# A recurrent scan on TensorE: the last 64 state channels packed, and the group norm moved to GpSimd

## The chip, the core and the metric

The kernel runs on one core of a Trainium2 chip. The metric is the time of one execution on the device in microseconds (us), as the median of several runs; lower is better.

## What is computed

The input `x` has 16 images of 56 x 56 pixels with 192 channels. Two blocks follow each other, each added to its input: a window block with a recurrence and a small two-layer network, and then a shifted-window attention block. The change touches only the first, which is, cut down:

```
g   = group_norm(x)                      # 32 groups of 6 channels
w   = layer_norm(windows of 7 x 7 of g) * ln1_w + ln1_b
h_t = w_t @ Bm + h_{t-1} @ A             # over the 49 tokens of a window
r   = h @ Cm
y   = layer_norm(r) * ln2_w + ln2_b
x1  = x + r + gelu(y @ W1 + b1) @ W2 + b2
```

There are 16 x 64 = 1024 windows. Each of the 49 tokens needs the state of the token before it.

## The kernel before

Stage 1 goes through the recurrence in slots. A slot works on one token of half of the windows: four tiles of 128 windows, 512 columns (`NTOK`), with 192 channels split into a part of 128 and a part of 64 (`CB`). With two halves and 49 tokens there are 98 tokens-by-half to do, and they are staggered: slot n computes the state of n+1, the network of n, and the normalised input of n+2. The instructions of each engine stand in the order in which the function `slot` of that engine writes them; engines meet only through semaphores (`wait_ge`, `then_inc`).

Matmuls want more exactness than one pass of the `float32r` format gives, so each operand is split into an upper part (the value as rounded to `float32r`, written by ScalarE) and a lower part (what is left, written mostly by VectorE). A product needs upper by upper, upper by lower and lower by upper. The class `Split` keeps four weight arrays, `a_hi, a_lo` for channels 0 to 127 and `b_hi, b_lo` for the last 64. For the last 64 channels of the data the upper part lies on partitions 0 to 63 and the lower on 64 to 127 of one tile (`hi[:, 1, :]`), and the weights stand there twice, so that one matmul does both. A product by a 192-row weight is thus five matmuls (`terms`), for each block of output columns.

On TensorE a slot is, in order: the scan (L623, 20 matmuls of 512 columns, 10 for the first 128 state channels and 10 for the last 64, into `ps_h`), the transposes of `yb` (L594, L596), the second half of the second layer of n-1 (L608), the first layer (L639, 30 matmuls), the mix `h @ Cm` (L650), the transposes of `xn`, and the first half of the second layer (L608). VectorE makes the lower parts `h_lo`, `y_lo`, `xn_lo` and four of six `g_lo`, the group norm (L505, L507), both layer norms' statistics and the residual sums; GpSimd makes two `g_lo`, the powers `rsa` and `rsb`, the sum `res` and the accumulators `acc_x`, `acc_x2`. SyncE's queue carries, per slot, one load `xt` (L374) and 14 stores of `x1`.

Names of the prediction: `y_lo` and `y_hi` must be complete before the first layer starts (`s_yl`), `xn_lo` and `xn_hi` before the scan (`s_xl`), and `g_lo` before the first half of the second layer (`s_gld`, `s_glp`).

Of the kernel before, what the change touches and what calls it, by code (L numbers as in the profile page):

```python
# [7 lines left out]
fp32 = mybir.dt.float32  # L8
# [15 lines left out]
P = 128  # L24
CB = C - P
# [31 lines left out]
def build(nc, x, A, Bm, Cm, ln1, ln2, W1, b1, W2, b2,  # L57
# [6 lines left out]
    with top:  # L64
# [31 lines left out]
        with ExitStack() as ctx:  # L96
# [8 lines left out]
            W_B, W_A, W_C = (Split(ctx, name, C) for name in ("wB", "wA", "wC"))  # L105
            W_1 = Split(ctx, "w1", HID)
# [8 lines left out]
            with ExitStack() as pre:  # L115
# [34 lines left out]
                def _(act):  # L150
# [9 lines left out]
                    for full, parts in ((fold_B, W_B), (raw_A, W_A), (raw_C, W_C), (fold_1, W_1)):  # L160
                        for t in range(2):
                            act.activation(parts.parts[2 * t][:, :], full[:, t, :], ACT.Copy)
                    act.activation(w2[:, :, 0, :], raw_2[:, :, :], ACT.Copy).then_inc(s_wh, 1)

                @block.gpsimd
                def _(pool):
# [17 lines left out]
                def _(dve):  # L184
# [30 lines left out]

                    dve.wait_ge(s_sum, 1)
# [64 lines left out]
            yb = sb("yb", [P, TPC, C])  # L281
            y_hi, y_lo = sb("y_hi", [P, 2, NTOK], f32r), sb("y_lo", [P, NTOK], f32r)
# [31 lines left out]
            s_t1, s_xh, s_xl = sem("xn_transposed"), sem("xn_hi_ready"), sem("xn_lo_ready")  # L314
            s_scan, s_hh, s_hl = sem("scan_summed"), sem("h_hi_ready"), sem("h_lo_ready")
# [73 lines left out]
            def _(act):  # L389
                act.wait_ge(s_init, 1)  # L390

                def upper_parts(hi, full):
                    act.activation(hi[:, 0, :], full[:, 0, :], ACT.Copy)
                    return act.activation(hi[0:CB, 1, :], full[0:CB, 1, :], ACT.Copy)

                def slot(t, c):
                    n = CHUNKS * t + c
                    if there(n + 1):

                        d = 1 - c  # L400
                        act.wait_ge(s_scan, n + 2)
                        upto(act, s_cm, n)
                        for k, rows in enumerate((P, CB)):
                            last = act.activation(h_hi[d][0:rows, k, :], ps_h[0:rows, k, :], ACT.Identity,  # L404
                                                  bias=hbias[0:rows, k:k + 1])
                        last.then_inc(s_hh, 1)
                    if there(n):
                        act.wait_ge(s_t2, n + 1)
                        upper_parts(y_hi, ps_g).then_inc(s_yh, 1)
# [14 lines left out]
                    if there(n + 2):  # L424
                        act.wait_ge(s_t1, n + 3)
                        upto(act, s_scan, n + 1)
                        upper_parts(xn_hi[c], ps_h).then_inc(s_xh, 1)
# [50 lines left out]
            def _(dve):  # L478
                def lower_parts(hi, lo, full, bias=None):

                    for k, rows, dst in ((0, P, lo[:, :]), (1, CB, hi[CB:P, 1, :])):
                        src, up = full[0:rows, k, :], hi[0:rows, k, :]
                        if bias is None:
                            last = dve.tensor_tensor(dst, src, up, ALU.subtract)
                        else:
                            last = dve.scalar_tensor_tensor(out=dst, in0=src, scalar=bias[0:rows, k:k + 1], in1=up,
                                                            op0=ALU.add, op1=ALU.subtract)
                    return last
# [911 lines left out]
```

## Time and profile before

| | us |
|---|---|
| median of 3 runs (4489.57 to 4497.21) | 4492.04 |
| the profiled execution | 4493.39 |
| its span | 4491.6 |
| TensorE busy, share of the span | 4286.1, 95% |
| VectorE busy | 3938.4, 88% |
| GpSimd busy | 2584.4, 58% |
| ScalarE busy | 2479.7, 55% |

### The profile page before, as it was taken

What the parts mean: (1) busy time and instruction counts of PE and PEld (TensorE: products, weight loads), DVE (VectorE), ACT (ScalarE), POOL (GpSimd) and SP (SyncE); (2) the same over time, 40 slices, a digit from 0 to 9 for tenths busy, and PEclk for the clock granted to TensorE, in tenths of its full rate; (3) what the DMA queues carried; (4) which work ended last, traced back from release to release, by engine and by line L of the source; (5) the groups of instructions that cost most, each with busy time, mean ns of one, the idle gap of its engine ahead of it and who ended that gap; (6) DMA issues with size and microseconds to landing.
All of it is one profiled execution on the core that took longest, in us unless ns stands there. A gap on an engine that the chain in (4) does not pass through costs nothing. (4 is left out here: it accounts for less than half of the span.)

```text
span 4491.6 us, 141866 instructions
## 1 busy us (share of the span) xinstructions
PE 4286.1 (95%) x52040; PEld 3664.5 (82%) x52040; DVE 3938.4 (88%) x8102; ACT 2479.7 (55%) x4852; POOL 2584.4 (58%) x2092
## 2 busy tenths in 40 slices
PE   0699999999999999999996999999999999999999
PEld 0588888888888888888885888888888888888887
DVE  8688888888888888888884999999899899999998
ACT  0244444444444444444442777777777777777776
POOL 0255554445545545555444777777767767777766
PEclk9999999999999999999997999999999999999999
DMA  8011111111111111111111222222222222222222
GB/s 362 23 40 40 40 40 37 38 39 39 39 39 39 39 40 40 40 40 40 37 39 41 78 77 76 76 78 76 77 75 75 76 77 75 77 76 76 79 76 64
DMA packets 390776, 284.66 MB, mean 63 GB/s; under 512 B 148159, under 2 KB 389188, under 8 KB 389700
## 3 DMA queue, kind: packets, MB, share of 16 engines
q1 hardware_dynamic: 387612, 281.57, 21.6%
q10 hardware_dynamic: 3112, 2.39, 0.2%
q8 instruction: 34, 0.56, 0.1%
q14 instruction: 18, 0.15, 0.0%
HBM read 119.00 MB, written 87.31 MB: 46 GB/s over the span
## 5 line engine op out<-in xcount | busy, mean ns | idle before, releaser
L904 POOL TENSOR_TENSOR L<-L,mx 128x588 f32<-128x588 f32 x512 | 600.2, 1172 | 596.1 <-DVE mx L1127 596.1
L608 PE MATMUL ps_o<-w,g_hi 128*128 128x384 f32 x2352 | 710.9, 365 | 5.9 <-DVE g_lo L548 4.1
L418 ACT ACTIVATE gF<-ps_g,b1f 128x512 f32<-128x512 f32 x588 | 406.2, 691 | 393.8 <-PE ps_g L639 391.3
L898 POOL TENSOR_TENSOR E<-E,ri 128x588 f32<-128x588 f32 x512 | 600.2, 1172 | 0.8 <-DVE ri L1133 0.8
L608 PE MATMUL ps_o<-w,g_lo 128*128 128x192 f32 x2352 | 534.3, 254 | 0.0
L447 POOL TENSOR_TENSOR res<-xt,b2b 128x768 f32<-128x768 f32 x98 | 181.0, 1847 | 590.9 <-DVE x L496 590.9
L1189 PE MATMUL ps_s<-Kp,Q 32*64 32x98 f32 x12288 | 493.6, 258 | 21.9 <-issue 18.8
L404 ACT ACTIVATE h_hi<-ps_h,hbias 128x512 fp32r<-128x512 f32 x196 | 123.2, 680 | 703.2 <-PE ps_h L623 703.2
L1011 ACT ACTIVATE o_hi<-ps_v,vb 128x98 fp32r<-128x98 f32 (+1 forms) x1024 | 290.2, 335 | 300.6 <-PE ps_v L1302 292.8
L608 PEld LDWEIGHTS ps_o<-w,g_hi 128*128 128x128 f32 x2352 | 429.3, 189 | 27.1 <-issue 25.1
L608 PEld LDWEIGHTS ps_o<-w,g_lo 128*128 128x128 f32 x2352 | 443.7, 191 | 0.0
L1123 DVE SCALAR_TENSOR_TENSOR L<-ps_s,bias 128x588 f32<-128x588 f32 x512 | 394.7, 771 | 55.0 <-PE ps_s L1189 37.6
L1127 DVE TENSOR_REDUCE mx<-L 128x12 f32<-128x588 f32 x512 | 392.2, 766 | 17.5
L986 ACT ACTIVATE PT<-ps_t 98x588 f32<-98x588 f32 x512 | 343.3, 670 | 112.2 <-PE ps_t L1265 109.2
L1302 PEld LDWEIGHTS ps_v<-PT,Vx 98*32 98x32 f32 x12288 | 310.5, 150 | 93.9 <-issue 64.3
L1131 DVE TENSOR_REDUCE sm<-E 128x12 f32<-128x588 f32 x512 | 386.5, 755 | 0.1
L1189 PEld LDWEIGHTS ps_s<-Kp,Q 32*64 32x64 f32 x12288 | 299.0, 130 | 103.3 <-issue 27.6
L1302 PE MATMUL ps_v<-PT,Vx 98*32 98x49 f32 x12288 | 374.6, 235 | 2.6 <-DVE o_hi L1108 1.3
L457 POOL TENSOR_TENSOR g_lo<-gF,g_hi 128x512 fp32r<-128x512 f32 x196 | 251.0, 1301 | 199.7 <-ACT g_hi L423 199.7
L423 ACT ACTIVATE g_hi<-gF 128x512 fp32r<-128x512 f32 x588 | 355.7, 622 | 0.0
L992 ACT ACTIVATE E<-L 128x588 f32<-128x588 f32 x512 | 351.3, 686 | 3.9 <-POOL L L904 0.8
L541 DVE TENSOR_SCALAR xn<-xn,mva,rsa 128x192 f32<-128x192 f32 x392 | 318.4, 875 | 2.3 <-POOL rsa L452 2.3
(220 smaller groups left out, 12446.9 us busy)
## 6 DMA issues: line engine op xcount, KB each, us to landing
xs<-in_x SPq DMA_DIRECT2D x8, 4704.0 KB, 22.7
xt<-in_x SPq DMA_DIRECT2D x98, 384.0 KB, 3.4
xb<-x_cells SPq DMA_DIRECT2D x128, 294.0 KB
Vx<-V SPq DMA_DIRECT2D x512, 73.5 KB
out<-yo SPq DMA_DIRECT2D x128, 294.0 KB
x_cells<-x SPq DMA_DIRECT2D x780, 48.0 KB
Kp<-K SPq DMA_DIRECT2D x256, 98.0 KB, 2.0
Kp<-K SPq DMA_DIRECT2D x256, 49.0 KB, 2.2
```

What stands on the lines that cost most here:

```text
L418: act.activation(gF[f % 4][:, :], ps_g[:, f % 2, :], ACT.Gelu, bias=b1f[:, f:f + 1]).then_inc(s_gelu, 1)
L423: act.activation(g_hi[:, g, :], gF[g % 4][:, :], ACT.Copy).then_inc(s_gh, 1)
L608: last = pe.matmul(dst, g[:, f, P * k:P * (k + 1)], w, start=(f == 0 and i == 0), stop=(f == FT - 1 and i == 1))
L898: pool.tensor_tensor(e, e, ri[p][:, :].unsqueeze(2).to_broadcast([P, HEADS, T]), ALU.mult)\
L904: pool.tensor_tensor(l, l, mx[p][:, :].unsqueeze(2).to_broadcast([P, HEADS, T]), ALU.subtract).then_inc(s_sub, 1)
L986: act.activation(PT[lp % 2][0:T2, :, :].rearrange("p j (w t) -> p w j t", w=2), ps_t[0:T2, :, 0:JP * SLOT].rearrange("p w (j t) -> p w j t ...
L992: act.activation(E[pp][:, :, :], L[pp][:, :, :], ACT.Exp).then_inc(s_ex, 1)
L1123: dve.scalar_tensor_tensor(out=L[p][:, :, :].rearrange("p (a h) m -> p a (h m)", a=2), in0=ps_s[:, :, 0:SB], scalar=HD ** -0.5, in1=tab, o ...
L1127: dve.tensor_reduce(mx[p][:, :], L[p][:, :, :], AX.X, ALU.max).then_inc(s_mx, 1)
L1131: dve.tensor_reduce(sm[pp][:, :], E[pp][:, :, :], AX.X, ALU.add).then_inc(s_sm, 1)
L1189: last = pe.matmul(s_pair(j)[SLOT * w:SLOT * (w + 1)], Q[c][rows, chunk, 2 * p + w, :], Kp[c][rows, chunk, :, 2 * p + w, :], start=True, s ...
L1302: last = pe.matmul(ps_v[row:row + 2 * HD, col:col + T], Vx[lc][0:T2, 2 * lp + w, g:2 * HD * JP:JP], PT[lp % 2][0:T2, j, T * w:T * (w + 1)] ...
```

## The change

Five things change in stage 1. First, the scan for the last 64 channels: the upper and the lower weights of these 64 output columns stand side by side in one stationary operand of 128 columns (`pack_B`, `pack_A`), so that one matmul gives the product by the upper weights on partitions 0 to 63 of `ps_h[:, 1]` and that by the lower weights on 64 to 127. ScalarE copies the upper half of the partitions into `h_b`, and VectorE adds the two halves. Second, for the first 128 state channels, the lower weights of the last 64 input rows of B and of A are joined in one operand (`W_AB_b_lo`), whose data operand `xh_b` is put together by two ScalarE copies. The scan has 15 matmuls in place of 20, with the packed ones first. Third, the two group-norm operations move from the head of VectorE's slot to the head of GpSimd's. Fourth, lower parts are released one by one, so that the first can start while the second upper part is still being made. Fifth, VectorE's order: `xn` (now L562) goes ahead of `g_lo` 0 and 1, and `g_lo` 4 and 5 go behind the second layer norm's statistics; TensorE takes the first half of the second layer in three pieces, each with its own wait.

```diff
                     if there(n + 1):
 
                         d = 1 - c
-                        pe.wait_ge(s_xl, n + 2)
-                        upto(pe, s_hl, n)
-                        for m, rows in enumerate((P, CB)):
-                            cols = slice(P * m, P * m + rows)
-                            terms = (*W_B.terms(xn_hi[d], xn_lo[d], cols), *W_A.terms(h_hi[d], h_lo[d], cols))
-                            for k, (w, v) in enumerate(terms):
-                                last = pe.matmul(ps_h[0:rows, m, :], w, v, start=(k == 0), stop=(k == len(terms) - 1))
+                        pe.wait_ge(s_xl, 2 * n + 4)
+                        pe.wait_ge(s_xs, n + 2)
+                        upto(pe, s_hl, 2 * n)
+                        upto(pe, s_hs, n)
+                        state = ((W_B, pack_B, xn_hi[d], xn_lo[d]), (W_A, pack_A, h_hi[d], h_lo[d]))
+                        for k, (w, pack, hi, lo) in enumerate(state):
+                            pe.matmul(ps_h[:, 1, :], pack[:, 0, :], hi[:, 0, :], start=(k == 0), stop=False)
+                            pe.matmul(ps_h[0:CB, 1, :], w.parts[0][:, P:C], lo[:, :], start=False, stop=False)
+                            last = pe.matmul(ps_h[:, 1, :], pack[:, 1, :], hi[:, 1, :], start=False, stop=(k == 1))
+                        last.then_inc(s_pack, 1)
+                        cols = slice(0, P)
+                        terms = (*W_B.terms(xn_hi[d], xn_lo[d], cols)[0:4], *W_A.terms(h_hi[d], h_lo[d], cols)[0:4],
+                                 (W_AB_b_lo[:, :], xh_b[d][:, :]))
+                        for k, (w, v) in enumerate(terms):
+                            last = pe.matmul(ps_h[:, 0, :], w, v, start=(k == 0), stop=(k == len(terms) - 1))
                         last.then_inc(s_scan, 1)
...
                     if there(n):
                         upto(pe, s_x1, n)
+                        pe.wait_ge(s_gld, len(LO_DVE) * n + 2)
+                        second_layer(0, (0, 1))
+                        pe.wait_ge(s_glp, len(LO_POOL) * (n + 1))
+                        second_layer(0, LO_POOL)
                         pe.wait_ge(s_gld, len(LO_DVE) * (n + 1))
-                        pe.wait_ge(s_glp, len(LO_POOL) * (n + 1))
-                        second_layer(0).then_inc(s_w2a, 1)
+                        second_layer(0, (4, 5)).then_inc(s_w2a, 1)
...
                     if there(n + 1):
 
                         d = 1 - c
+                        act.wait_ge(s_pack, n + 2)
+                        act.activation(h_b[:, :], ps_h[CB:P, 1, :], ACT.Copy).then_inc(s_hu, 1)
                         act.wait_ge(s_scan, n + 2)
                         upto(act, s_cm, n)
-                        for k, rows in enumerate((P, CB)):
-                            last = act.activation(h_hi[d][0:rows, k, :], ps_h[0:rows, k, :], ACT.Identity,
-                                                  bias=hbias[0:rows, k:k + 1])
-                        last.then_inc(s_hh, 1)
+                        act.activation(h_hi[d][:, 0, :], ps_h[:, 0, :], ACT.Identity,
+                                       bias=hbias[:, 0:1]).then_inc(s_hh, 1)
+                        act.wait_ge(s_hb, n + 2)
+                        act.activation(h_hi[d][0:CB, 1, :], h_b[:, :], ACT.Identity,
+                                       bias=hbias[0:CB, 1:2]).then_inc(s_hh, 1)
...
+                        act.wait_ge(s_xh, 2 * n + 6)
+                        act.activation(xh_b[c][0:CB, :], xn_hi[c][0:CB, 1, :], ACT.Copy).then_inc(s_xs, 1)
+                    if there(n + 1):
+                        act.wait_ge(s_hh, 2 * n + 4)
+                        act.activation(xh_b[1 - c][CB:P, :], h_hi[1 - c][0:CB, 1, :], ACT.Copy).then_inc(s_hs, 1)
...
+                    if there(n + 2):
+
+                        pool.wait_ge(s_x[c], 16 * (t + 2))
+                        upto(pool, s_t1, n + 1)
+                        r = slice(TPC * c, TPC * (c + 1))
+                        pool.tensor_tensor(xn[c][:, :, :], xt[c][:, :, :], R1[:, r, :], ALU.mult).then_inc(s_gs, 1)
+                        pool.wait_ge(s_gs, n + 3)
+                        pool.tensor_tensor(xn[c][:, :, :], xn[c][:, :, :], M1[:, r, :],
+                                           ALU.subtract).then_inc(s_gn, 1)
...
+                        dve.wait_ge(s_hu, n + 2)
+                        dve.tensor_tensor(h_b[:, :], ps_h[0:CB, 1, :], h_b[:, :], ALU.add).then_inc(s_hb, 1)
+                        dve.wait_ge(s_hh, 2 * n + 3)
+                        dve.scalar_tensor_tensor(out=h_lo[d][:, :], in0=ps_h[:, 0, :], scalar=hbias[:, 0:1],
+                                                 in1=h_hi[d][:, 0, :], op0=ALU.add, op1=ALU.subtract).then_inc(s_hl, 1)
+                        dve.wait_ge(s_hh, 2 * n + 4)
+                        dve.wait_ge(s_hb, n + 2)
+                        dve.scalar_tensor_tensor(out=h_hi[d][CB:P, 1, :], in0=h_b[:, :], scalar=hbias[0:CB, 1:2],
+                                                 in1=h_hi[d][0:CB, 1, :], op0=ALU.add, op1=ALU.subtract)\
+                            .then_inc(s_hl, 1)
```

On TensorE, the second half of the scan before: the last two matmuls of 128 state channels and the ten of 64 (partitions x columns of the output stand behind the names).

```order
L623 MATMUL ps_h<-h_hi,wA_b_hi 128x512
L623 MATMUL ps_h<-h_hi,wA_b_lo 128x512
L623 MATMUL ps_h<-xn_hi,wB_a_hi 64x512
L623 MATMUL ps_h<-xn_lo,wB_a_hi 64x512
L623 MATMUL ps_h<-xn_hi,wB_a_lo 64x512
L623 MATMUL ps_h<-xn_hi,wB_b_hi 64x512
L623 MATMUL ps_h<-xn_hi,wB_b_lo 64x512
L623 MATMUL ps_h<-h_hi,wA_a_hi 64x512
L623 MATMUL ps_h<-h_lo,wA_a_hi 64x512
L623 MATMUL ps_h<-h_hi,wA_a_lo 64x512
L623 MATMUL ps_h<-h_hi,wA_b_hi 64x512
L623 MATMUL ps_h<-h_hi,wA_b_lo 64x512
```

The scan of the changed kernel from its first matmul; four more of line L657 follow, the last of them on `xh_b` and `wAB_b_lo`.

```order
L649 MATMUL ps_h<-xn_hi,pack_B 128x512 [waits h_lo_ready,h_b_hi_stacked,xn_b_hi_stacked,xn_lo_ready]
L650 MATMUL ps_h<-xn_lo,wB_a_hi 64x512
L651 MATMUL ps_h<-xn_hi,pack_B 128x512
L649 MATMUL ps_h<-h_hi,pack_A 128x512
L650 MATMUL ps_h<-h_lo,wA_a_hi 64x512
L651 MATMUL ps_h<-h_hi,pack_A 128x512
L657 MATMUL ps_h<-xn_hi,wB_a_hi 128x512
L657 MATMUL ps_h<-xn_lo,wB_a_hi 128x512
L657 MATMUL ps_h<-xn_hi,wB_a_lo 128x512
L657 MATMUL ps_h<-xn_hi,wB_b_hi 128x512
L657 MATMUL ps_h<-h_hi,wA_a_hi 128x512
```

The last 64 channels now come first, in six matmuls, and the output's width changes four times within the scan where it changed once.

On VectorE, the stretch from the mix to the next scan, before: the statistics of the second layer norm (`s6b`, `mvb`, `veb`) and the lower parts that the scan waits for.

```order
L548 TENSOR_TENSOR g_lo<-gF,g_hi 128x512 [waits hidden_hi_ready] x2
L554 BN_STATS s6b<-ps_r 128x6 [waits mixed]
L554 BN_STATS s6b<-ps_r 128x6 x3
L559 BN_AGGR mvb<-s6b 128x2 [waits ln2_stats,weights_loaded]
L559 BN_AGGR mvb<-s6b 128x2 x3
L562 TENSOR_SCALAR veb<-mvb 128x4 [waits ln2_aggregated]
L484 TENSOR_TENSOR xn_lo<-ps_h,xn_hi 128x512 [waits xn_hi_ready]
L484 TENSOR_TENSOR xn_hi<-ps_h,xn_hi 64x512
```

The same stretch of the changed kernel.

```order
L575 BN_STATS s6b<-ps_r 128x6 [waits mixed]
L575 BN_STATS s6b<-ps_r 128x6 x3
L580 BN_AGGR mvb<-s6b 128x2 [waits ln2_stats,weights_loaded]
L580 BN_AGGR mvb<-s6b 128x2 x3
L583 TENSOR_SCALAR veb<-mvb 128x4 [waits ln2_aggregated]
L588 TENSOR_TENSOR g_lo<-gF,g_hi 128x512 [waits hidden_hi_ready] x2
L517 TENSOR_TENSOR xn_lo<-ps_h,xn_hi 128x512 [waits xn_hi_ready]
L517 TENSOR_TENSOR xn_hi<-ps_h,xn_hi 64x512 [waits xn_hi_ready]
```

The pair of `g_lo` moved from ahead of the wait for the mix to behind it, between the statistics and `xn_lo`.

On GpSimd, the head of the changed slot; before, `res` stood directly behind the second `acc_x` row.

```order
L504 TENSOR_TENSOR acc_x<-acc_x,x 128x768
L507 TENSOR_TENSOR acc_x<-acc_x,x1sq 128x768 [waits x1_squared]
L472 TENSOR_TENSOR xn<-xt,R 128x768 [waits xn_transposed,x_loaded0]
L474 TENSOR_TENSOR xn<-xn,M 128x768 [waits gn_scaled]
L481 TENSOR_TENSOR res<-xt,b2b 128x768 [waits x1_ready,gn_scaled]
L486 TENSOR_TENSOR rsa<-vea,neg_half 128x4 [waits ln1_var_eps]
```

Two operations on 768 columns stand between the accumulators and `res`, and the first of them waits for the load of `xt`.

## Rows read from the trace of the kernel before

**Rows 1.** Windows by stage: start, us, busy us (x instructions) per engine, clock, DMA.
```profile
170.00:2385.00 2215.00, 2209.65 (x12972) 1903.54 (x12971) 1957.78 (x4152) 1006.94 (x1747) 1108.76 (x771) 1.00 0.14 38
...
2385.00:4491.00 2106.00, 2044.43 (x38946) 1734.98 (x38945) 1853.83 (x3622) 1463.97 (x3089) 1452.90 (x1295) 0.99 0.27 75
```

**Rows 2.** Waits, 300 to 2100 us: us in total, times, longest.
```profile
DVE xn L505 <- DMA xt<-in_x: 64.5, 79, 1.1
...
PEld ps_g L639 <- DVE y_hi L484: 20.5, 79, 0.3
```

**Rows 3.** Timeline of TensorE, one slot: start, us, engine, line, operation.
```profile
1011.81 0.39 PE L623 MATMUL ps_h<-xn_hi,wB_a_hi 128*128 128x512 f32 x1
...
1016.17 0.39 PE L623 MATMUL ps_h<-h_hi,wA_b_lo 128*64 128x512 f32 x1
...
1016.40 0.60 PE L594 MATMUL ps_g<-ident,yb 128*128 128x128 f32 x4
...
1017.19 0.42 PE L608 MATMUL ps_o<-w,g_hi 128*128 128x384 f32 x1
...
1020.87 0.50 PE L639 MATMUL ps_g<-y_hi,w_a_hi 128*128 128x512 f32 x1
...
1027.90 0.25 PE L650 MATMUL ps_r<-wC_a_hi,h_hi 128*128 128x192 f32 x1
...
1030.00 0.27 PE L650 MATMUL ps_r<-wC_b_lo,h_hi 128*128 128x192 f32 x1
...
1030.11 0.60 PE L594 MATMUL ps_h<-ident,xn 128*128 128x128 f32 x4
...
1031.07 0.44 PE L608 MATMUL ps_o<-w,g_hi 128*128 128x384 f32 x1
...
1034.61 0.39 PE L623 MATMUL ps_h<-xn_hi,wB_a_hi 128*128 128x512 f32 x1
```

**Rows 4.** Timeline of VectorE around the same slot.
```profile
1006.88 1.28 DVE L548 TENSOR_TENSOR g_lo<-gF,g_hi 128x512 fp32r<-128x512 f32 x2
...
1008.08 1.15 DVE L554 BATCH_NORM_STATS2 s6b<-ps_r 128x6 f32<-128x192 f32 x4
...
1010.52 0.68 DVE L484 TENSOR_TENSOR xn_hi<-ps_h,xn_hi 64x512 fp32r<-64x512 f32 x1
...
1014.23 0.56 DVE L496 TENSOR_TENSOR x<-ps_o,x 128x384 f32<-128x384 f32 x1
...
1015.50 1.38 DVE L505 TENSOR_TENSOR xn<-xt,R 128x768 f32<-128x768 f32 x1 [0.71 <-DMA xt<-in_x]
...
1020.13 0.68 DVE L484 TENSOR_TENSOR y_hi<-ps_g,y_hi 64x512 fp32r<-64x512 f32 x1
...
1021.50 0.56 DVE L496 TENSOR_TENSOR x<-ps_o,x 128x384 f32<-128x384 f32 x1
```

**Rows 5.** Timeline of GpSimd, same stretch.
```profile
1010.00 1.01 POOL L461 TENSOR_TENSOR rsb<-veb,neg_half 128x4 f32<-128x4 f32 x1 [3.16 <-DVE veb L562]
...
1014.22 1.85 POOL L473 TENSOR_TENSOR acc_x<-acc_x,x1sq 128x768 f32<-128x768 f32 x1
...
1022.13 1.85 POOL L447 TENSOR_TENSOR res<-xt,b2b 128x768 f32<-128x768 f32 x1 [6.07 <-DVE x L496]
```

**Rows 6.** Timeline of SyncE's DMA queue, and the queue's row of the page.
```profile
1023.10 11.20 SPq L363 DMA_DIRECT2D x_cells<-x  x14
...
1035.00 0.44 SPq L374 DMA_DIRECT2D xt<-in_x  x1
...
xt<-in_x SPq DMA_DIRECT2D x98, 384.0 KB, 3.4
```

**Rows 7.** ScalarE's h_hi: its group on the page, mean ns; then its timeline row.
```profile
L404 ACT ACTIVATE h_hi<-ps_h,hbias 128x512 fp32r<-128x512 f32 x196 | 123.2, 680 | 703.2 <-PE ps_h L623 703.2
...
1016.60 1.26 ACT L404 ACTIVATE h_hi<-ps_h,hbias 128x512 fp32r<-128x512 f32 x2 [7.16 <-PE ps_h L623]
```

**Rows 8.** Line L541, 300 to 2100 us: duration ns min/median/max.
```profile
L541 DVE TENSOR_SCALAR xn<-xn,mva,rsa x315: 373/381/1435, 319.2 to 2099.4; 128x192 f32<-128x192 f32 x158
```

More of the change, by code:

```diff
@@ L162, in _ @@
                             act.activation(parts.parts[2 * t][:, :], full[:, t, :], ACT.Copy)
+                    for full, pack in ((fold_B, pack_B), (raw_A, pack_A)):
+                        for t in range(2):
+                            act.activation(pack[:, t, 0:CB], full[:, t, P:C], ACT.Copy)
                     act.activation(w2[:, :, 0, :], raw_2[:, :, :], ACT.Copy).then_inc(s_wh, 1)
@@ L214, in _ @@
                                                   in1=sq[:, 0, :], op0=ALU.mult, op1=ALU.add))
+                    dve.wait_ge(s_wh, 1)
+                    for full, parts, rows in ((fold_B, W_B, slice(0, CB)), (raw_A, W_A, slice(CB, P))):
+                        dve.tensor_tensor(W_AB_b_lo[rows, :], full[rows, 1, 0:P], parts.parts[2][rows, 0:P],
+                                          ALU.subtract)
                     dve.wait_ge(s_sum, 1)
@@ L281, in build @@
             yb = sb("yb", [P, TPC, C])
+            xh_b = [sb(f"xh_b{b}", [P, NTOK], f32r) for b in range(2)]
+            h_b = sb("h_b", [CB, NTOK])
             y_hi, y_lo = sb("y_hi", [P, 2, NTOK], f32r), sb("y_lo", [P, NTOK], f32r)
@@ L478, in _, with lower_parts @@
             def _(dve):
-                def lower_parts(hi, lo, full, bias=None):
+                def lower_parts(hi, lo, full, upper, count, ready):
                     for k, rows, dst in ((0, P, lo[:, :]), (1, CB, hi[CB:P, 1, :])):
[L482 to L488, printed above, removed]
+                        dve.wait_ge(upper, count + k - 1)
+                        dve.tensor_tensor(dst, full[0:rows, k, :], hi[0:rows, k, :], ALU.subtract).then_inc(ready, 1)
                 def x1_half(b, half, partial, count):
@@ L531, in slot @@
                         dve.tensor_scalar(vea[:, :], mva[:, :, 1], LN_EPS, None, ALU.add).then_inc(s_ve1, 1)
-                    if there(n):
-                        for f in LO_DVE[:2]:
-                            dve.wait_ge(s_gh, FT * n + f + 1)
-                            dve.tensor_tensor(g_lo[:, f, :], gF[f % 4][:, :], g_hi[:, f, :], ALU.subtract)\
-                                .then_inc(s_gld, 1)
-                    if there(n + 2):
                         dve.wait_ge(s_rs1, n + 3)
@@ L597, in transposes, with second_layer @@
                     return last
-                def second_layer(half):
+                def second_layer(half, blocks=range(FT)):
                     for k in (2 * half, 2 * half + 1):
-                        for f in range(FT):
+                        for f in blocks:
                             both = (ps_o[:, k % 2, 0:2 * C], g_hi, w2[:, f, :, :].rearrange("p a c -> p (a c)"))
```

50 lines of the change are left out of this document (26 added, 24 removed).

## The prediction

> **What bounds the kernel now.** I read the windows by stage first [rows 1]. Stage 1, which the change touches, fills 170 to 2385 us, and TensorE is busy for 2209.65 us of that 2215. VectorE has 1957.78, GpSimd 1108.76, ScalarE 1006.94. So a gain has to come out of TensorE's slot, and VectorE is near enough (88%) to take it back. The second stage runs the same instructions before and after, and I give it nothing.
>
> Next, one slot on TensorE's timeline [rows 3]. It runs from the first scan matmul at 1011.81 to the next at 1034.61: 22.80 us. There are 98 of them (x98) [rows 6], so 97 intervals. Inside it: scan 4.59 (to 1016.40), transposes 0.79, second half of the second layer 3.68, first layer 7.03, mix 2.21, transposes 0.96, first half of the second layer 3.54. Twenty scan matmuls in 4.59 is 0.2295 each, start to start.
>
> Two of these pieces contain waits. The second layer takes 3.68 in one half and 3.54 in the other, and the first layer takes 7.03 for 30 matmuls that need 30 x 0.23 = 6.90. That is 0.27 together, and the view of waits names it: weight loads of the first layer waited for `y_hi` 79 times, 0.26 us each [rows 2]. The last lower part ended at 1020.81 [rows 4], the first layer began at 1020.87. The other wait is at the transposes of `xn`, 0.96 against 0.79: the second layer needs `g_lo` 5, which ended at 1008.16 in the slot before [rows 4]. So 22.80 is some 22.36 of matmuls and 0.44 of waits.
>
> **The change, part by part.** I count from the first scan matmul, S = 0.
>
> *Scan.* Fifteen matmuls in place of twenty: 15 x 0.2295 = 3.44, so 1.15 less. A packed matmul is 128 wide, and the width does not change the price: twenty of both widths keep one spacing, the step from 64 wide back to 128 wide included (1016.17 to 1016.40, 0.23) [rows 3]. The change has four changes of width in the scan. Bounds: nothing, by that row; at most a full wait for the matmul ahead, 0.39 - 0.23 = 0.16 each. I take nothing. The Trainium skill, TensorEngine Tiling (Array Packing), Key Properties, says that a change of tiling mode drains TensorE, which would speak against this scan. The row between 64 and 128 wide shows no such gap; by the rule the scan would cost the rival's price below.
>
> *TensorE without a wait.* 3.44 + 0.79 = 4.23; second layer 3.54 to 7.77; first layer 6.90 to 14.67; mix 2.21 to 16.88; transposes 0.79 to 17.67; second layer 3.54 to 21.21. That is the floor, 1.59 under 22.80.
>
> *What is late next.* Between the end of the mix and the next scan TensorE has only 0.79 + 3.54 = 4.33 of work, and VectorE's new order puts everything in there. Before, `g_lo` 4 and 5 stood ahead of the wait for the mix (1006.88 to 1008.08) and cost TensorE 0.17. Now the chain is: the mix's last matmul ends 0.16 after its slot time (1030.00 + 0.27 against 1030.11) [rows 3], 0.05 to get across, then statistics to the end of `xn_hi`, 1008.08 to 1011.20 = 3.12 [rows 4], with the pair of `g_lo` inside, another 1.20, and 0.06 to TensorE (as `y_hi` to the first layer). Sum 4.59, so the next scan starts at 16.88 + 4.59 = 21.47. The last third of the second layer waits for `g_lo` 5 on the way, but that lies within the same time. Of the floor's gain 0.26 goes here.
>
> *The way from scan to first layer.* This was tight before and the change alters it most. The last scan matmul starts at 3.21 and ends at 3.60; `h_hi`'s first part goes from 3.64 (the 0.04 of 1016.56 to 1016.60) to 4.32 [rows 7]. VectorE comes from its last sum, which ended 3.59 after `xn_hi` (1011.20 to 1014.79) [rows 4], at 3.53 here; it adds `h_b` to 4.21, and `h_lo` ends at 5.11 (three lower parts take 1017.86 to 1020.13, 0.76 each [rows 4, 7]). ScalarE's `h_b` copy (0.68 at most, by `h_hi`'s mean) fits between the packed part, over at 1.54, and 3.53. Then comes the lower part of the last 64 channels, L539. Both its inputs lie in SBUF, and GpSimd will be in the group norm. When is that? `x1`'s second half ends 1.33 behind the second layer (1022.06 against 1020.73) [rows 3, 4], so at 9.10; the load `xt` is issued 12.94 later (1035.00, behind 14 stores of 11.20) and lands in 3.4 [rows 6]: 25.44, which is 3.8 in the next slot. The accumulators end 6.07 after `rsb` starts (1010.00 to 1016.07) [rows 5]; that is about 3.5. So the first norm operation runs from 3.9 to 5.75 if it takes 1.85, as `acc_x2` does [rows 5]. Bounds: 1.38, VectorE's own time for it, to 2.4 if VectorE holds it up by 0.55.
>
> What happens when they meet is in the rows. L505 read two SBUF tiles and started at 1015.50 under GpSimd's `acc_x2`, which ended at 1016.07; it ended at 1016.88, 0.81 later [rows 4, 5]. Likewise L541 has a median of 381 ns and a maximum of 1435 [rows 8]. So I let L539 wait for the norm's end and then take 512/768 of 0.81: 5.75 + 0.54 = 6.29. `y_lo` and `y_hi` follow to 7.7, against 7.77 when TensorE wants them. The Trainium skill, SBUF — State Buffer, Who interferes with whom, has the same as a rule: a VectorE instruction with two SBUF inputs contends with a GpSimd one that reads SBUF, and the second to issue blocks until the first is done. The trace agrees by that 0.81; a reader who thought of port sharing as a slight slowdown would put L539 at 5.9 and see no danger. The 0.27 wait for `y_hi` is thus just gone, with nothing to spare. I put 0.1 for it and 0.08 for restarts of TensorE after its wait at the scan.
>
> *Hidden.* The norm on GpSimd is up to 3.7 in place of VectorE's 2.4; it sits in GpSimd's idle 6.07 before `res` [rows 5] and ends by 7.6 to 8.2, ahead of the statistics at 9.1. Without that cover `xn` would be late by the excess. `res` then runs 9.17 to 11.02, `rsa` to 12.1, the four `xn` (now with GpSimd idle, 0.38 each at most) to 13.6, `g_lo` 0 and 1 (1.28 for a pair) to 15.0; TensorE needs them at 17.67. The fifth gelu waits for `g_lo` 0 until 14.3 instead of 13.7; its upper part is wanted at about 18.9. The two `xh_b` copies on ScalarE come after `xn_hi` is transposed (18 plus 4 x 0.68 = 20.7), before 21.5. Filling the pipeline costs some longer GpSimd steps and the packing of weights six small operations: 3 us once.
>
> *Sum.* 21.47 + 0.18 = 21.65 a slot, 1.15 less than 22.80. 97 x 1.15 = 112; the profiled execution's 4493.4 - 112 + 3 = 4384. It stood 1.4 above the median of the runs, so 4383 there.
>
> **Rivals.**
> *No wait left (0.10).* The chain behind the mix may be shorter than I add up, since it was taken with gaps of other waits in it. Then the floor holds: 97 x 1.59 = 154, 4493.4 - 154 + 3 - 1.4 = 4341. Against it: statistics, `g_lo` and `xn` lower parts are 4.3 of pure work.
> *The scan drains at changes of width (0.10).* 2 changes more a slot than before (four and none behind it, against one and one) at 0.16 is 0.32 with everything behind it: 97 x 0.32 = 31, so 4414. For it: a packed and a 64-wide matmul in one accumulation do not occur in this trace. Against: the 0.23.
> *The state's lower part misses its gap (0.10).* If the first norm operation ends before L539 is ready at 5.11, the second takes the port for 1.85. With an end at 5.3 and L539 later still (a late `h_hi`): 7.15, L539 to 7.7, `y_hi` to 9.1, first layer at 9.2 instead of 7.77, slot 9.2 + 6.90 + 2.21 + 4.59 + 0.15 = 23.05. That is 0.25 longer than before: 97 x 0.25 = 24, and 4516. It decides at 0.64 us, the distance from 5.11 to 5.75; a load landing that much earlier or a state that much later does it. This is the slower case. Another 0.03 goes to slower by a wait I don't see.
> *The gain is eaten to within 0.2% (0.05):* a mixture of late `y_hi` and late `g_lo`, slot 22.75.
>
> **How the numbers follow.** My forecast, 4365 to 4410, has 0.62. The measurement of this kernel tells about 0.2% (9 us) from no change. Faster: 0.62 + 0.10 + 0.10 = 0.82; same 0.05; slower 0.13. The range 4345 to 4440 takes in the forecast, the drain at twice its price and most of the way to the floor.
>
> **What the profile of after would show.** Scan matmuls 0.23 apart across widths, or gaps of 0.16 there. A slot of 21.65. TensorE idle by 0.2 to 0.4 ahead of the last third of the second layer and of the scan, `xn` lower parts ending just before the scan. L539 at 1.1 to 1.3 us, ending 0.54 after the first norm operation. `xn` (L562) at 0.38 throughout. The first norm operation starting 3.8 after the scan. If L539 ends after the second norm operation and the first layer waits over 1 us for `y_hi`, the slower rival holds; if TensorE has no waits, the floor does.

## The result, and the profile after

The changed kernel takes 4386.88 us (median of 4 runs, 4384.31 to 4396.41) against 4490.81 us in the runs beside it: a ratio of 0.977, with a 95% interval of 0.9751 to 0.9788. The prediction said 4383. The profiled execution took 4384.42 us, where the prediction's sum had 4384. One of the six executions of e8 below, at 13239.63 us, is left out as slow.

The head of its page: the span, then busy us, share and instructions of each engine.

```profile
span 4382.6 us, 142449 instructions
...
PE 4170.2 (95%) x51550; PEld 3612.2 (82%) x51550; DVE 3617.6 (83%) x8006; ACT 2658.1 (61%) x5150; POOL 3076.1 (70%) x2292
```

VectorE fell from 88% to 83%, GpSimd rose from 58% to 70%, TensorE stayed at 95%. The windows by stage, cut where stage 1 ends now, answer to [rows 1].

```profile
175.00:2282.00 2107.00, 2096.51 (x12473) 1853.56 (x12474) 1635.36 (x4057) 1182.77 (x2034) 1588.64 (x961) 1.00 0.15 40
2282.00:4382.00 2100.00, 2040.67 (x38957) 1730.98 (x38956) 1854.50 (x3622) 1461.24 (x3089) 1453.06 (x1295) 0.99 0.27 75
```

The second stage takes what it took. TensorE is still busy in nearly all of stage 1. The slot's length can be read from the starts of one scan matmul; this row is line L649 between 300 and 2100 us (count, duration in ns, first and last start).

```profile
L649 PE MATMUL ps_h<-xn_hi,pack_B x83: 466/473/504, 300.1 to 2082.2; 128*128 128x512 f32 x83
```

82 intervals between 300.1 and 2082.2 us make 21.73 us a slot, where it was 22.81. The two halves of the loop now differ: slots of about 21.6 and 21.86 us take turns. One slot on TensorE's timeline, to lay beside [rows 3]:

```profile
995.58 0.47 PE L649 MATMUL ps_h<-xn_hi,pack_B 128*128 128x512 f32 x1
995.89 0.39 PE L650 MATMUL ps_h<-xn_lo,wB_a_hi 128*64 128x512 f32 x1
996.12 0.39 PE L651 MATMUL ps_h<-xn_hi,pack_B 128*128 128x512 f32 x1
996.35 0.39 PE L649 MATMUL ps_h<-h_hi,pack_A 128*128 128x512 f32 x1
...
999.10 0.60 PE L620 MATMUL ps_g<-ident,yb 128*128 128x128 f32 x4
...
999.89 0.42 PE L634 MATMUL ps_o<-w,g_hi 128*128 128x384 f32 x1
...
1003.40 0.39 PE L673 MATMUL ps_g<-y_hi,w_a_hi 128*128 128x512 f32 x1
...
1012.50 0.60 PE L620 MATMUL ps_h<-ident,xn 128*128 128x128 f32 x4
...
1013.29 0.42 PE L634 MATMUL ps_o<-w,g_hi 128*128 128x384 f32 x1
...
1015.55 0.25 PE L634 MATMUL ps_o<-w,g_lo 128*128 128x192 f32 x1
1015.82 0.44 PE L634 MATMUL ps_o<-w,g_hi 128*128 128x384 f32 x1
...
1017.14 0.50 PE L649 MATMUL ps_h<-xn_hi,pack_B 128*128 128x512 f32 x1
```

The four changes of width in the scan leave no gap: 995.89, 996.12 and 996.35 lie 0.23 apart through 64, 128 and 128 columns. Only the first matmul behind a wait is slow (995.58 to 995.89, 0.31; at 1017.14, in the other half of the loop, 0.34). The scan takes 3.52, transposes 0.79, the second half of the second layer 3.51, first layer and mix 9.10. In the first half of the second layer the third piece starts at 1015.82, 0.27 behind its last neighbour instead of 0.09, and the next scan at 1017.14. The view of waits puts names to the two (us in total, times, longest):

```profile
PEld ps_o L634 <- DVE g_lo L588: 20.7, 82, 0.3
PEld ps_h L649 <- issue: 13.5, 42, 0.4
PEld ps_h L649 <- DVE xn_hi L517: 6.7, 41, 0.2
```

`g_lo` 5 costs the weight loads 0.25 a slot. The scan's weight loads wait 0.16 for `xn_hi` in one half of the loop. In the other they stand idle for 0.32, put down to "issue", which is time for which the profile shows no cause. VectorE over the same slot, answering to [rows 4]:

```profile
1000.02 0.75 DVE L535 SCALAR_TENSOR_TENSOR h_lo<-ps_h,hbias,h_hi 128x512 fp32r<-128x512 f32 x1 [0.48 <-ACT h_hi L421]
1000.80 0.92 DVE L539 SCALAR_TENSOR_TENSOR h_hi<-h_b,hbias,h_hi 64x512 fp32r<-64x512 f32 x1
...
1002.47 0.68 DVE L517 TENSOR_TENSOR y_hi<-ps_g,y_hi 64x512 fp32r<-64x512 f32 x1
1003.60 0.56 DVE L522 TENSOR_TENSOR x<-ps_o,res 128x384 f32<-128x384 f32 x1 [0.45 <-PE ps_o L634]
...
1007.91 1.25 DVE L562 TENSOR_SCALAR xn<-xn,mva,rsa 128x192 f32<-128x192 f32 x4 [1.13 <-POOL rsa L486]
...
1012.70 1.16 DVE L575 BATCH_NORM_STATS2 s6b<-ps_r 128x6 f32<-128x192 f32 x4 [2.33 <-PE ps_r L684]
...
1014.47 1.29 DVE L588 TENSOR_TENSOR g_lo<-gF,g_hi 128x512 fp32r<-128x512 f32 x2
...
1016.40 0.68 DVE L517 TENSOR_TENSOR xn_hi<-ps_h,xn_hi 64x512 fp32r<-64x512 f32 x1
```

And GpSimd, answering to [rows 5]:

```profile
997.51 1.86 POOL L507 TENSOR_TENSOR acc_x<-acc_x,x1sq 128x768 f32<-128x768 f32 x1
999.33 1.83 POOL L472 TENSOR_TENSOR xn<-xt,R 128x768 f32<-128x768 f32 x1
1001.24 2.17 POOL L474 TENSOR_TENSOR xn<-xn,M 128x768 f32<-128x768 f32 x1
...
1009.48 3.29 POOL L491 TENSOR_TENSOR g_lo<-gF,g_hi 128x512 fp32r<-128x512 f32 x2 [1.60 <-ACT g_hi L442]
1014.62 1.41 POOL L495 TENSOR_TENSOR rsb<-veb,neg_half 128x4 f32<-128x4 f32 x1 [1.86 <-DVE veb L583]
```

These rows show the two engines at the port that they share. L539 was ready at 1000.80 while GpSimd's L472 ran to 1001.16; it ended at 1001.72, 0.56 behind it. In turn L474 started under L539 and took 2.17, where it takes 1.83 to 1.86 in e4 and e6, and `rsb`, which began under two `g_lo`, took 1.41 where it took 1.01. `h_lo` (L535), with one input from PSUM, ran wholly under L472 and took 0.75, as it does with GpSimd idle in e6. `xn` runs in 1.25 in place of 3.25; GpSimd is idle then (1007.88 to 1009.48), where it was in `g_lo` before. `y_hi` ended at 1003.15, 0.25 before the first layer at 1003.40: no wait there. L472 followed directly on `acc_x2` (997.51 + 1.86); between 300 and 2100 us it waited for the load of `xt` in two slots, for 0.4 us in all.

### The profile page after: what moved, and what is told of

Its sections match the earlier page's. It is cut to its first block and busy times, and to the rows that moved or that the text cites. A ratio compares the mean times of both kernels' runs of the same rounds, so it can differ in the third digit from the quotient of the medians.

```text
span 4382.6 us, 142449 instructions
## 1 busy us (share of the span) xinstructions
PE 4170.2 (95%) x51550; PEld 3612.2 (82%) x51550; DVE 3617.6 (83%) x8006; ACT 2658.1 (61%) x5150; POOL 3076.1 (70%) x2292
## 5 line engine op out<-in xcount | busy, mean ns | idle before, releaser
L634 PE MATMUL ps_o<-w,g_hi 128*128 128x384 f32 x2352 | 722.9, 367 | 5.3 <-DVE g_lo L588 1.9
L491 POOL TENSOR_TENSOR g_lo<-gF,g_hi 128x512 fp32r<-128x512 f32 x196 | 314.2, 1622 | 172.7 <-ACT g_hi L442 172.7
L575 DVE BATCH_NORM_STATS2 s6b<-ps_r 128x6 f32<-128x192 f32 x392 | 113.5, 352 | 235.8 <-PE ps_r L684 235.8
L1302 PE MATMUL ps_t<-ident,E 64*98 64x64 f32 x6144 | 277.5, 223 | 0.0
```

Source lines behind the costliest of these rows:

```text
L634: last = pe.matmul(dst, g[:, f, P * k:P * (k + 1)], w, start=(f == 0 and i == 0), stop=(f == FT - 1 and i == 1))
L1302: last = pe.transpose(ps_t[0:T2, w, SLOT * j:SLOT * (j + 1)], E[lp][rows, 2 * j:2 * j + 2, :].rearrange("p h m -> p (h m)"), ident[rows, r ...
```

## The experiments

Each slot below is read as for the changed kernel, from the first and last start of a scan matmul between 300 and 2100 us. The runs fall in three groups, each with its own runs of the kernel before: 4490.26 us for e1 to e4, 4493.15 for e5 to e8, 4493.76 for e9 and e10. Every ratio is to the group's own; a difference of 3 us across groups means nothing.

| run | what is different | us | slot, us |
|---|---|---|---|
| before | | 4490 to 4494 | 22.81 |
| changed | | 4386.9 | 21.73 |
| e1 | norm at the head of VectorE's slot | 4528.2 | 23.28 |
| e2 | changed, with the scan of 20 matmuls | 4487.7 | 22.77 |
| e3 | `g_lo` 4 ahead of the mix | 4399.6 | 21.83 |
| e4 | 0.69 us more before L539 | 4590.7 | 23.87 |
| e5 | `g_lo` 5 on GpSimd | 4381.6 | 21.69 |
| e6 | norm waits for L539 | 4388.9 | 21.75 |
| e7 | e5 and e6 together | 4341.2 | 21.24 |
| e8 | no 64-wide matmul in the scan | 4389.8 | 21.75 |
| e9 | e7 with the scan of 20 | 4448.4 | 22.40 |
| e10 | e5, and the norm on VectorE behind `y_hi` | 4426.8 | 22.16 |

### e1: the norm back on VectorE

```diff
 (GpSimd's slot)
-                    if there(n + 2):
-
-                        pool.wait_ge(s_x[c], 16 * (t + 2))
-                        ...
 (head of VectorE's slot)
+                    if there(n + 2):
+
+                        dve.wait_ge(s_x[c], 16 * (t + 2))
+                        upto(dve, s_t1, n + 1)
+                        r = slice(TPC * c, TPC * (c + 1))
+                        dve.tensor_tensor(xn[c][:, :, :], xt[c][:, :, :], R1[:, r, :], ALU.mult).then_inc(s_gs, 1)
+                        dve.wait_ge(s_gs, n + 3)
+                        dve.tensor_tensor(xn[c][:, :, :], xn[c][:, :, :], M1[:, r, :],
+                                          ALU.subtract).then_inc(s_gn, 1)
```

> The changed kernel with the two group-norm operations back at the head of VectorE's slot; all the rest as changed. Theory P (a slot is TensorE's matmuls plus the waits that the chains through ScalarE and VectorE leave): the norm cannot start before xt lands, 3.75 us after the scan begins, and h_b, h_lo, h_hi, y_lo, y_hi stand behind it on VectorE, so y_hi ends at about 9.3 instead of 7.6 and the first layer waits about 1.5. Slot about 23.1 us, time about 4520 us: slower than the kernel before, although its scan has five matmuls fewer. Rival Q (the packed scan is worth its five matmuls wherever the norm stands, since VectorE has over 10% of idle time): slot about 21.7 to 21.9, time 4385 to 4405.

4528.18 us, ratio 1.0091 (1.0076 to 1.0106): slower than the kernel before, with five matmuls fewer in each slot. Its waits:

```profile
ACT h_hi L424 <- DVE h_b L533: 146.3, 78, 2.0
PEld ps_g L673 <- DVE y_hi L508: 118.9, 77, 1.6
...
DVE xn L525 <- DMA xt<-in_x: 2.2, 10, 0.3
```

The second `h_hi` waits 1.88 for `h_b`, which stands behind the norm, and the first layer's weight loads 1.54 for `y_hi`. Rival Q falls: the packed scan alone lengthens the way from scan to first layer by an operation on each of two engines, and with the norm on that way the slot loses more than the matmuls give. The expected 4520 was 8 short. The edit shows the cost of the norm's two operations at that place; e10 puts them at another.

### e2: the scan of 20 matmuls in the changed kernel

```diff
-                        state = ((W_B, pack_B, xn_hi[d], xn_lo[d]), (W_A, pack_A, h_hi[d], h_lo[d]))
-                        ...
+                        for m, rows in enumerate((P, CB)):
+                            cols = slice(P * m, P * m + rows)
+                            terms = (*W_B.terms(xn_hi[d], xn_lo[d], cols), *W_A.terms(h_hi[d], h_lo[d], cols))
+                            for k, (w, v) in enumerate(terms):
+                                last = pe.matmul(ps_h[0:rows, m, :], w, v, start=(k == 0), stop=(k == len(terms) - 1))
```

The edit also takes out the operations on `h_b` and `xh_b`, which are not shown.

> The changed kernel with the scan of 20 matmuls, no h_b and no copies into xh_b; norm on GpSimd, the finer releases and VectorE's new order stay. Theory P: the wait of the first layer for y_hi goes away (0.27 a slot), and the wait behind the mix comes (about 0.26 against 0.17 before); slot about 22.6 to 22.65, 97 x 0.15 to 0.2 us less than before, time 4470 to 4477 us, so that the packing alone is worth about 90 us of the 104 when the rest is there. Rival Q (it is the relief of VectorE that made the gain): time below 4440 us.

4487.71 us, ratio 0.9997 (0.9988 to 1.0006): no difference, where Theory P said 4470 to 4477, 15 to 20 us less than before. The norm's move, the finer releases and the new order together win 0.04 a slot. The wait at the first layer went, and the tail gave the same back:

```profile
PEld ps_o L623 <- DVE g_lo L577: 20.2, 79, 0.3
PEld ps_h L638 <- DVE xn_hi L509: 12.7, 79, 0.2
```

Both waits, 0.26 and 0.16 a slot, are in the tail that VectorE's order has filled. So the gain is not in the relief of VectorE by itself; and Theory P had weighed the tail (the stretch from the mix to the next scan) too lightly. Nor is it in the packing by itself: with the norm on VectorE's way (e1) the packed scan is 38 us slower than the kernel before. e1 and e2 each take one of the two away, and neither is faster than the kernel before; with both the kernel is 104 us faster.

### e3: one `g_lo` ahead of the wait for the mix

```diff
-                        for f in LO_DVE[:2]:
+                        for f in LO_DVE[:3]:
 ...
-                        for f in LO_DVE[2:]:
+                        for f in LO_DVE[3:]:
```

> The changed kernel with g_lo 4 ahead of VectorE's wait for the mix, where VectorE is idle for 2.4 us, and only g_lo 5 behind the statistics. Theory P says that the chain of statistics, two g_lo and two xn lower parts (4.6 us against 4.33 of TensorE work) ends the slot, so taking 0.65 out of it moves TensorE's wait at the next scan and at the last third of the second layer to nothing: slot 21.72 to 21.35 or less, time down by 25 to 40 us to about 4350, unless the shorter slot brings the group norm later against the scan (xt is issued a fixed time behind x1) and y_hi eats part of it. Rival R (the waits seen at the scan are the price of the loop and of the queues, not of VectorE's chain): no change within 5 us.

4399.61 us, ratio 0.9799 (0.9786 to 0.9812): about 13 us slower than the changed kernel, where 25 to 40 faster were expected. The timeline shows where it went. GpSimd, with its `g_lo` and, a slot on, the first norm operation:

```profile
1012.88 2.93 POOL L491 TENSOR_TENSOR g_lo<-gF,g_hi 128x512 fp32r<-128x512 f32 x2 [1.96 <-ACT g_hi L442]
...
1024.61 1.85 POOL L472 TENSOR_TENSOR xn<-xt,R 128x768 f32<-128x768 f32 x1
```

VectorE, with `g_lo` 4, and in the next slot L539 and `y_hi`:

```profile
1015.22 1.13 DVE L569 TENSOR_TENSOR g_lo<-gF,g_hi 128x512 fp32r<-128x512 f32 x1 [1.82 <-ACT g_hi L442]
...
1025.38 1.63 DVE L539 SCALAR_TENSOR_TENSOR h_hi<-h_b,hbias,h_hi 64x512 fp32r<-64x512 f32 x1
...
1027.76 0.69 DVE L517 TENSOR_TENSOR y_hi<-ps_g,y_hi 64x512 fp32r<-64x512 f32 x1
```

`g_lo` 4 was ready at 1015.22 and ended at 1016.35, 0.54 behind GpSimd's pair (1015.81). The transposes behind the mix began at 1015.91, so the statistics began 0.17 later behind it than in the changed kernel (1016.28, against 1012.70 behind 1012.50). The next scan came at 1020.23, 4.32 behind the mix in place of 4.64. Both bring the norm later against the scan, since it follows the statistics through `veb`, `rsb` and the accumulators, and GpSimd waits for nothing between `rsb` and the norm: L472 began 4.38 behind the scan (3.75 to 3.92 in the changed kernel) and ended at 1026.46, L539 took 1.63 and ended at 1027.01, `y_hi` at 1028.45. The clause "unless `y_hi` eats part of it" came true and more, though not by the load of `xt`, for which the norm never waits here. TensorE had no wait left in the tail and a new one at the first layer (45.0 us in 83 slots for its weight loads). The slot is now the time once round this chain, from the statistics over GpSimd's accumulators and norm, L539, `y_hi`, the first layer and its lower parts back to the statistics: 1016.28 to 1038.11, 21.83. Rival R expected no change within 5 us and falls; that the waits in the tail went shows them to be VectorE's chain.

### e4: the state's lower part made later

```diff
+                        dve.tensor_tensor(junk[:, :], ps_h[:, 0, :], h_hi[d][:, 0, :], ALU.subtract)
                         dve.wait_ge(s_hh, 2 * n + 4)
                         dve.wait_ge(s_hb, n + 2)
```

> The changed kernel with one more VectorE operation of 128x512 from PSUM (0.69 us) into a tile that nobody reads, between h_lo and the lower part of the last 64 channels (L539). Theory P with the shared port: L539 is ready at about 5.95 instead of 5.22 us after the scan's start, after the first norm operation ends (5.6), so the second takes the port first and L539 waits for its end, about 7.45; y_hi ends at about 9.3 and the first layer waits 1.3 to 1.5. Slot about 23.0 to 23.2, time about 4510 to 4525: 0.7 us of work costs 1.4. Rival S (two engines that share a port only slow each other a little): L539 takes at most 1.0, y_hi ends at 8.3, slot 22.0 to 22.3, time 4415 to 4440.

4590.7 us, ratio 1.0224 (1.0209 to 1.024). GpSimd's two norm operations:

```profile
1027.47 1.85 POOL L473 TENSOR_TENSOR xn<-xt,R 128x768 f32<-128x768 f32 x1
1029.39 1.83 POOL L475 TENSOR_TENSOR xn<-xn,M 128x768 f32<-128x768 f32 x1
```

and VectorE's L539, here L541:

```profile
1029.54 2.23 DVE L541 SCALAR_TENSOR_TENSOR h_hi<-h_b,hbias,h_hi 64x512 fp32r<-64x512 f32 x1
```

It was ready 0.15 behind the start of the second norm operation, waited for its end (1031.22) and took 0.55 more. That is the rival of the prediction, made to happen: 0.7 us of work costs 2.1 a slot. Rival S falls. Theory P said 4510 to 4525, and its mechanism holds while its size does not. The wait of the first layer was larger than its 1.3 to 1.5: for the weight loads 140.6 us in 75 slots or 1.87 each.

```profile
PEld ps_g L675 <- DVE y_hi L518: 140.6, 75, 2.0
```

The second norm operation ended 7.49 to 7.67 behind the scan's start, in turn by halves of the loop, where 7.45 was taken, and `y_hi` at 9.49 to 9.66 where 9.3 was. The first layer began at 9.54 to 9.72, against 7.82 to 7.87 in the changed kernel: 1.7 to 1.9 later. In 14 slots a clock loss came on top, which is below.

### e5, e6, e7: each end of the slot, and both

e5 gives `g_lo` 5 to GpSimd, e6 adds one wait, e7 has both:

```diff
-            LO_DVE, LO_POOL = (0, 1, 4, 5), (2, 3)
+            LO_DVE, LO_POOL = (0, 1, 4), (2, 3, 5)
 ...
-                        pe.wait_ge(s_glp, len(LO_POOL) * (n + 1))
-                        second_layer(0, LO_POOL)
+                        pe.wait_ge(s_glp, len(LO_POOL) * n + 2)
+                        second_layer(0, (2, 3))
                         pe.wait_ge(s_gld, len(LO_DVE) * (n + 1))
+                        pe.wait_ge(s_glp, len(LO_POOL) * (n + 1))
```

```diff
                         upto(pool, s_t1, n + 1)
+                        upto(pool, s_hl, 2 * n + 4)
```

> The changed kernel with g_lo 5 made by GpSimd behind g_lo 3, where it is idle for 1.9 us; VectorE keeps g_lo 4 behind the statistics. The chain behind the mix loses 0.65 and the statistics are not late. Theory P with the shared port: the tail shrinks from 4.64 to TensorE's 4.33, but with the shorter slot the first norm operation, tied to x1 through the stores and xt, ends 0.3 later against the scan (6.0 to 6.1), L539 is held to 6.6, and y_hi ends at 8.05 instead of 7.62, so the first layer waits 0.2 to 0.3. Slot 21.5 to 21.65, time 4362 to 4380. Rival N (no port between them): slot 21.35, time about 4350.

> The changed kernel with one more wait: the first norm operation on GpSimd starts only when L539 has ended (the port is free for it). Theory P: L539 takes 0.75 instead of 0.95 to 1.06, y_hi ends at 7.4 instead of 7.6 to 7.76; the first layer had no wait for it (7.83), so nothing is won; the norm ends at 9.65, behind the 9.13 at which the statistics want it, and VectorE has 2.4 us of idle time behind to absorb the 0.5. Time within 5 us of the changed kernel (4383 to 4392). A rival in which the shared port costs the changed kernel something on its path: 10 us or more faster.

> Both edits: g_lo 5 on GpSimd and the norm behind L539. Theory P: the tail is TensorE's 4.33, and y_hi ends at 7.4 whatever the load does, so neither end of the slot waits. Slot 21.3 to 21.4, time 4348 to 4358; that is more than e5 and e6 give together, which is the mark of two waits of which one hides behind the other. Rival N: as e5, or a little worse by the later norm.

e5: 4381.61 us, ratio 0.9751 (0.9739 to 0.9764). e6: 4388.9 us, 0.9768 (0.9755 to 0.978). e7: 4341.22 us, 0.9665 (0.9653 to 0.9678). Against the changed kernel e5 is 5 us faster (8 by the ratios, whose intervals overlap) and e6 no faster; together they are worth 46 (47 by the ratios). e6 came as expected. e5 lies just above its 4362 to 4380 and far from rival N's 4350; e7 lies 7 us below its 4348 to 4358. In e5 the wait moved to the first layer, 0.43 a slot:

```profile
PEld ps_g L673 <- DVE y_hi L517: 35.2, 82, 0.5
...
1017.83 1.86 POOL L472 TENSOR_TENSOR xn<-xt,R 128x768 f32<-128x768 f32 x1
...
1018.75 1.49 DVE L539 SCALAR_TENSOR_TENSOR h_hi<-h_b,hbias,h_hi 64x512 fp32r<-64x512 f32 x1
```

The scan of that slot began at 1013.61, so the norm's first operation ended 6.08 behind it and L539 6.63, as expected. But no row has the norm wait for the load, as the expectation had it; it starts where the accumulators end, as in e3. The wait in the tail was hiding this one: it kept the scan late enough for the norm to be done.

In e7 TensorE waits for no engine between 300 and 2100 us; the one row of its loads is this, and below it the slot's row.

```profile
PEld ps_h L650 <- issue: 4.0, 19, 0.2
```

```profile
L650 PE MATMUL ps_h<-xn_hi,pack_B x84: 389/391/475, 317.9 to 2081.2; 128*128 128x512 f32 x84
```

83 intervals between 317.9 and 2081.2 us: 21.24. The prediction had added up 21.21 for a slot without waits, and its rival "no wait left" had 4341 us.

### e8: one width

```diff
-                            pe.matmul(ps_h[0:CB, 1, :], w.parts[0][:, P:C], lo[:, :], start=False, stop=False)
+                            pe.matmul(ps_h[:, 1, :], pack[:, 0, :], lo[:, :], start=False, stop=False)
```

> The changed kernel with the two 64-wide matmuls of the packed part made 128 wide (the packed weights on the lower part of the data, which adds the product of lower by lower to the sum): no change of width is left in the scan. If a change of width drained TensorE by 0.16, four of them gone would save 0.6 a slot, 60 us. Theory P: they cost nothing, time within 5 us of the changed kernel.

4389.84 us, ratio 0.9768 (0.9755 to 0.978), against 0.977 for the changed kernel; 60 us less would have been seen. Changes of width cost nothing here.

### e9: e7 with the scan of 20 matmuls

The edits of e2, e5 and e6 together.

> The kernel of e7 (g_lo 5 on GpSimd, the norm behind the state's lower part) with the scan of 20 matmuls, as in e2. If nothing waits at either end of the slot, the two scans differ by five matmuls and nothing else: slot 21.25 + 5 x 0.2295 = 22.40, time 4341 + 97 x 1.15 = 4452 us, within 8. Then of e7's 152 us under the kernel before the packing is 111 and the two ends of the slot 41. Rival Q (the relief of VectorE and the order carry the gain, the matmuls hide behind others): below 4425.

4448.41 us, ratio 0.9899 (0.9883 to 0.9914), within the 8 us given. The slot is 22.40, 1.16 above e7, and 5 x 0.2295 is 1.15. So where nothing waits, the packing is worth its five matmuls, 107 us, and the rest of e7's 152 us, 45, is in the waits. The rival of this run (below 4425) falls.

### e10: the norm on VectorE, behind `y_hi`

```diff
 (VectorE's slot)
                     if there(n):
                         lower_parts(y_hi, y_lo, ps_g, s_yh, 2 * n + 2, s_yl)
+                    if there(n + 2):
+
+                        dve.wait_ge(s_x[c], 16 * (t + 2))
+                        ...
```

The same two operations go from GpSimd's slot, as in e1, and `g_lo` 5 is on GpSimd as in e5.

> g_lo 5 on GpSimd as in e7, and the two norm operations back on VectorE, not at the head of its slot as in e1 but behind y_lo and y_hi. If it is the place on the way from the scan to the first layer that cost e1 its 37 us over the kernel before, and not VectorE's load, then here y_hi ends at 7.35 and is not late, the norm runs 7.4 to 9.3 with GpSimd idle, x1's second half ends at 10.4, the statistics of the first norm at 11.6, xn at 15.2 (wanted at 16.85), and g_lo 1 at 16.5, just before the mix ends. Slot 21.25 to 21.5, time 4341 to 4365. If VectorE's load is what matters: as e1, over 4450.

4426.76 us, ratio 0.9848 (0.9835 to 0.9862): neither of the two. The half about `y_hi` holds: the first layer has no wait, and 101 us of e1's time are back. How much of that is e5's edit, which was worth 5 to 8 us in the changed kernel, was not run apart. But the load returned later in the slot. `xn` now falls under GpSimd's first `g_lo`:

```profile
1000.63 2.24 DVE L562 TENSOR_SCALAR xn<-xn,mva,rsa 128x192 f32<-128x192 f32 x4 [1.14 <-POOL rsa L477]
```

It takes 2.24 where it took 1.25, `g_lo` 0 comes late, the fifth gelu waits 2.66 for its buffer, and `g_lo` 5 comes last of the lower parts that TensorE waits for in the tail:

```profile
ACT gF L437 <- DVE g_lo L569: 215.3, 81, 2.7
...
PE ps_o L634 <- POOL g_lo L482: 39.0, 81, 0.6
```

In one slot the way from the mix to the next scan is 5.19 (1004.06 to 1009.25) where TensorE's own work there is 4.33; that 0.86 is nearly all of the 0.92 by which the slot exceeds e7's.

## Why the prediction was right

**The scan.** "Fifteen matmuls in place of twenty, 1.15 less": e7 and e9 differ by 1.16. "I take nothing" for the changes of width: the 0.23 between rows of both widths and e8 agree. The rival that let the scan drain is out. The rule of the Trainium skill (TensorEngine Tiling (Array Packing), Key Properties), a drain when the tiling mode changes, does not carry over to a 64-wide matmul among 128-wide ones: no run here shows a drain, and none shows whether such a matmul changes the mode at all. The range was said to hold that rival at twice its price; twice 31 us would be 4445, just outside.

**The floor.** 21.21 was forecast for a slot without waits (the prediction's floor). e7 has 21.24.

**What is late next.** The chain behind the mix was put at 4.59, with the next scan at 21.47. From the transposes at 1012.50 to the scan at 1017.14 it took 4.64. The 0.18 for restarts and `y_hi` was meant as two terms, 0.08 and 0.1; `y_hi` cost nothing, and the restart cost more: the first scan matmul is 0.08 to 0.11 slow, and in one half of the loop it begins 0.25 behind `xn_hi` (1038.98 against 1038.73) where the other half has 0.06. Why the halves differ stays open. The sum stood at 21.65, measured 21.73.

**From scan to first layer.** The norm was to start at 3.9 and started at 3.75 (999.33 - 995.58), in the other half of the loop at 3.91. That the time came out is in part luck: the prediction had the load of `xt` set it, with the accumulators done at 3.5. They ended at about 3.8, since `rsb` took 1.41 in place of 1.01, and the load hardly ever held the norm. L539 was to end 0.54 behind the first norm operation and ended 0.54 to 0.56 behind; it took 0.92 to 1.04 in place of 1.1 to 1.3, since it was ready later than 5.11, at 5.22 to 5.27. The Trainium skill's rule on the shared port (SBUF — State Buffer, Who interferes with whom) and the traces agree in e3, e4 and the changed kernel: the second to start waits for the end of the first, and both directions occur. `y_hi` was to end at 7.7 and ended at 7.57 to 7.74, with the first layer at 7.82 to 7.87: the "nothing to spare" was 0.12 to 0.25.

**The slower rival.** It was priced at 4516 and had 0.10. e4 shows that it is there, but dearer (4591): the first layer was to begin at 9.2 and began at 9.54 to 9.72, and some 22 us of e4's time are the clock's. It was to be decided at 0.64 us; in the changed kernel L539 is ready 0.36 to 0.50 before the first norm operation ends.

**What was off.** The text gave the relief of the first layer 0.27 a slot. e2 has that relief and the new tail, and comes out 0.04 under the kernel before; the forecast for it (15 to 20 us) failed by taking the tail at 0.26 instead of the 0.42 of its two waits. In the prediction this hid in a sum that the packing dominates. The once-only term was set at +3. The span shrank by 109.0, of which the way from the first scan to the last holds 107. The first scan starts 5.1 later than before (150.5 against 145.4), and the rest outside that way is some 7 shorter, so that the term is about -2. Where the 7 come from was not traced. So the slots gave 107 of the forecast 112 and the once-only term 5 more than it was given: two errors of 5 us that cancel. That the sum's 4384 met the profiled 4384.42 to under 1 us is luck; the slot, right to 0.08 us, is not.

## What to carry to other kernels

When an engine is full and its instructions are cut, add up first the slot without waits, then the longest chain through other engines, be it between two pieces of the slot or, as in e3, once round from slot to slot; the longer sets the slot, but for the slow first matmul behind a wait. Two such chains can hide each other: e5 and e6 won 5 and nothing, e7 with both won 46, so an edit that "does nothing" is to be tried with the other end open. When VectorE and GpSimd both read SBUF, look at which instruction each can meet, and order them with a semaphore where a late part would wait behind a long one.

## What the runs showed of the hardware

The shared port gives cliffs. Of two GpSimd operations back to back (1029.32 and 1029.39, 0.07 apart) VectorE's L539 missed the gap when it was ready 0.15 late, and then paid for all that was left of the second one, 1.68. Ready before the first one ends, it goes ahead of the second (changed kernel, e3, e5). Alone it takes 0.75 (e6).

In e4, whose first-layer weight loads wait 1.87 us a slot, TensorE's clock fell in some slots, directly behind that wait: TensorE was busy for 1.00 us of the 2.70 from 911.00 to 913.70. The windows of e4: a slot without the loss, and the stretch of 3.3 us inside the slot before (start:end, length, busy us per engine, granted clock, DMA).

```profile
929.00:953.00 24.00, 22.33 (x131) 19.40 (x131) 19.10 (x44) 12.30 (x21) 16.20 (x12) 1.00 0.13 36
913.70:917.00 3.30, 3.30 (x8) 2.63 (x9) 2.83 (x11) 0.69 (x1) 2.04 (x2) 0.50 0.00 0
```

The granted clock is 0.50 of full speed there, the lower of the two levels (1.2 GHz). Fourteen of its 97 slots take 25.3 us instead of about 23.8, which is some 22 us of e4's time. The other slots have the same wait and keep the upper level, and no run shows what sets the fourteen apart. e1, whose wait there is 1.54 on average, stays at the upper level from 300 to 2100 us:

```profile
300.00:2100.00 1800.00, 1695.83 (x9976) 1481.92 (x9976) 1444.43 (x3400) 956.43 (x1621) 946.06 (x619) 1.00 0.14 38
```
